# Two layers of adaptive FFN and experts: expert weights split into halves in layer 0 and kept in HBM, conditioning loads merged and moved, routed products on VectorE

## The chip, the cores and the metric

One NeuronCore of one Trainium2 chip runs the whole program. The metric is the device time of one execution, in microseconds.

## What is computed

x is 32 sequences of 64 rows and 512 columns, 2048 tokens. Two residual layers follow each other:

```
x = x + L0_ffn(einsum('bct,bcd->bdt', x, W0[cond_b]))
x = x + L1_ffn(einsum('bct,bcd->bdt', x, W1[subj_b]) + side[subj_b][:, :, None])
```

L0_ffn has a dense FFN of 2048 hidden units with GELU and eight low-rank experts of rank 8 of which each token takes two; each of its two choices has its own hidden activation. L1_ffn has a shared gated FFN of 704 hidden units and eight experts of 352 hidden units, two a token:

```
scores = softmax(x @ gate_w);  topk_w, topk_idx = top_k(scores, 2)
g = silu(einsum('td,edh->teh', x, w_gate)) * einsum('td,edh->teh', x, w_up)
routed = einsum('teh,ehd,te->td', g, w_down, comb)
out = routed + silu(x @ sw_gate) * (x @ sw_up) @ sw_down
```

## The kernel before

The program is written engine by engine. Each engine has its own block with its instructions in order, and semaphores tie the blocks together. An instruction that waits holds everything behind it on its engine. SP only issues DMAs (queue q1). POOL issues DMAs too (queue q0) and does arithmetic.

**Split products.** Matmul operands are kept as two halves, hi (a cast to fp32r) and lo (the value minus hi). A product takes three matmuls: hi by hi, hi by lo, lo by hi. So most data pass a cast (ScalarE mostly) and a subtraction (VectorE or POOL).

**Layer 0** runs over four supers of 512 tokens (s = 0 to 3), and in each over 16 hidden tiles (f). A tile step of TensorE (`step`, L1704) is `hidden` of tile i (14 matmuls), `down` of tile i-1, first half (8), `second` of tile i (2), `down` second half (8). ScalarE does two gelus a tile, `gelu_first` (L894) and `gelu_second` (L900). VectorE does six operations, `hidden_tile` (L1199, L1202 to L1215). `down` waits for g_lo (L1210), `second` for the first gelu. In super 0 the weights come raw from HBM: ScalarE casts (L835), POOL subtracts (`low_w1`, L663), SP stores the split w1 tile to HBM (L505). From super 1 on SP reloads these halves (L513), one tile of 704 KB a step. SP's queue also holds the stores of x1 (L527, at f = 1 of the next super), the loads of xres (L487), of xt halves (L482) and, in super 3, of acc (L516, at f = 4 and 8).

At the turn from super to super VectorE has extra work between tile 0 and tile 1: `add_sums` (L1260) within tile 0 and `add_moved` (L1253) behind it; ScalarE has `move_sums` (L933) between its gelus of tile 1.

After its last `low_w1` POOL loads layer 1's conditioning: 32 matrices of 64 by 64 into `cw1` and 32 columns into `side_col` (`load_matrix`, L444, issues L449 and L452, in a hardware loop at L672). Then it is idle until super 3, where it loads the shared weights (`load_s`, L680).

**Layer 1** first runs the shared FFN over the four supers, with conditioning, gate, top-2 choice and the lists of slots in between. Then comes the routed stage: 39 slot tiles of 128 slots, sorted by expert. `slot_tile` of TensorE is: gate of t+1, `turn_g` of t (three transposes, L1941), up of t+1, `turn_x` of t+2 (four transposes, L1914), `down_routed` of t (L1953, L1954, L1958). Per tile ScalarE does seven operations: xg_hi and xg_f (L1002, L1005), silu (L1012), ru (L1016), rgt_hi and rgt_f (L1020, L1023) and the weighed output yt (L1030). Since POOL cannot read PSUM, xg_f, ru and rgt_f are plain copies of PSUM for it. POOL does `x_low` (L761), `products` (L769) and `g_low` (L773), and between them issues the gather of tile t+5 (L744) and the scatter-add of tile t-1 (L755). A scatter-add waits for the one before to land. VectorE splits the weights of the next expert (`split_expert`, L1469, L1477 to L1491) as soon as the last tile of the expert two before is done; SP loads them raw (`load_expert`, L605), 1408, 512 and 192 KB, when the split before is through.

## Time and profile before

| | us |
|---|---|
| runs | 1054.9, 2602.53, 1051.52 |
| median | 1054.9 |
| the profiled execution | 1050.06 |
| its span | 1048.2 |
| mean granted TensorE clock | 0.993 |

| engine | busy us | share |
|---|---|---|
| TensorE matmul | 1010.6 | 96% |
| TensorE weight load | 837.2 | 80% |
| VectorE | 524.3 | 50% |
| POOL | 354.5 | 34% |
| ScalarE | 314.4 | 30% |

Layer 0 fills the span up to about 540 us, the shared FFN up to about 755, the routed stage the rest. Times in a row are microseconds from the first instruction. In a row of the timeline the bracket gives the idle time of the engine before it and what ended it. A busy TensorE is not TensorE at its peak: the end of a matmul is modelled and overlaps the next one's start, so distances between starts tell the pace.

### The profile page before, as it was taken

What the parts mean: (1) busy time and instruction counts of PE and PEld (TensorE: products, weight loads), DVE (VectorE), ACT (ScalarE), POOL (GpSimd) and SP (SyncE); (2) the same over time, 40 slices, a digit from 0 to 9 for tenths busy, and PEclk for the clock granted to TensorE, in tenths of its full rate; (3) what the DMA queues carried; (4) which work ended last, traced back from release to release, by engine and by line L of the source; (5) the groups of instructions that cost most, each with busy time, mean ns of one, the idle gap of its engine ahead of it and who ended that gap; (6) DMA issues with size and microseconds to landing.
All of it is one profiled execution on the core that took longest, in us unless ns stands there. A gap on an engine that the chain in (4) does not pass through costs nothing.

```text
span 1048.2 us, 14852 instructions
## 1 busy us (share of the span) xinstructions
PE 1010.6 (96%) x4893; PEld 837.2 (80%) x4895; DVE 524.3 (50%) x886; ACT 314.4 (30%) x550; POOL 354.5 (34%) x351
## 2 busy tenths in 40 slices
PE   8899999999999999999999999999989999999993
PEld 5678887888888887888867777778778999999992
DVE  3788777455565455555566333665543314443000
ACT  3743332211121112111242010301144545454541
POOL 4123245410000000000042000022168889898873
PEclk9999999999999999999999999999999999999997
DMA  7387543443433434453444101005155665665433
GB/s 239 130 297 272 161 136 122 166 161 114 140 123 121 153 128 161 142 181 123 138 159 151 41 1 41 1 1 198 58 187 108 163 163 142 141 146 119 80 61 40
DMA packets 51322, 136.41 MB, mean 130 GB/s; under 512 B 8708, under 2 KB 10004, under 8 KB 50772
## 3 DMA queue, kind: packets, MB, share of 16 engines
q1 hardware_dynamic: 36660, 108.15, 30.1%
q0 software_dynamic: 12432, 25.71, 12.4%
q10 hardware_dynamic: 2192, 2.08, 0.7%
q8 instruction: 19, 0.31, 0.1%
q14 instruction: 19, 0.16, 0.0%
HBM read 96.85 MB, written 39.07 MB: 130 GB/s over the span
## 4 chain that ended last, share of the span: by engine, by line
PE 85%; DVE 4%; POOL 4%; DMA 2%; issue 1%; ACT 1%; ACTq 1%; PEldq 0%; POOLq 0%; PEld 0%; DVEq 0%
PE ps_y L1687 6%; PE ps_y L1689 6%; PE ps_y L1688 5%; PE ps_h L1645 5%; PE ps_h L1647 5%; PE ps_h L1646 5%; PE ps_u L1700 3%; PE ps_u L1699 3%; PE ps_h L1933 2%; PE ps_y L1933 2%; PE ps_y L1928 2%; PE ps_y L1929 2%; PE ps_y L1856 2%; PE ps_y L1857 2%; PE ps_h L1840 2%; PE ps_h L1841 2%
## 5 line engine op out<-in xcount | busy, mean ns | idle before, releaser
L1202 DVE TENSOR_TENSOR h<-h,wb 128x512 f32<-128x512 f32 x64 | 44.4, 693 | 162.6 <-ACT h L903 162.5
L897 ACT ACTIVATE h<-ps_h,bias 128x512 f32<-128x512 f32 x64 | 44.0, 689 | 235.1 <-PE ps_h L1654 235.1
L685 POOL DMA_DIRECT2D s_raw<-in_sgu x8 | 4.3, 544 | 299.9 <-DVE g_lo L1210 192.1
L1687 PE MATMUL ps_y<-w_hi,g_hi 128*128 (+1 forms) x256 | 102.2, 399 | 3.5 <-DVE g_lo L1210 3.5
L1689 PE MATMUL ps_y<-w_hi,g_lo 128*128 (+1 forms) x256 | 101.2, 395 | 0.0
L1688 PE MATMUL ps_y<-w_lo,g_hi 128*128 (+1 forms) x256 | 101.0, 395 | 0.0
L1645 PE MATMUL ps_h<-xt_hi,w_hl 128*128 128x512 f32 x256 | 100.0, 391 | 0.7 <-ACT lg_t L846 0.7
L1647 PE MATMUL ps_h<-xt_hi,w_hl 128*128 128x512 f32 x256 | 100.3, 392 | 0.0
L1646 PE MATMUL ps_h<-xt_lo,w_hl 128*128 128x512 f32 x256 | 100.2, 391 | 0.0
L1477 DVE CAST eg_hi<-e_raw 128x704 fp32r<-128x704 f32 x32 | 16.7, 581 | 138.0 <-PE ps_y L1958 125.3
L903 ACT ACTIVATE h<-ps_h,bias 128x512 f32<-128x512 f32 x64 | 43.9, 688 | 115.4 <-PE ps_h L1667 115.4
L755 POOL DMA_INDIRECT out_x<-yt,slot_tok x39 | 62.7, 1607 | 23.3 <-DMA out_x<-yt,slot_tok 12.5
L761 POOL TENSOR_TENSOR xg_lo<-xg_f,xg_hi 128x512 fp32r<-128x512 f32 x39 | 56.3, 1443 | 17.0 <-ACT xg_f L1005 14.9
L1687 PEld LDWEIGHTS ps_y<-w_hi,g_hi 128*128 128x128 f32 x256 | 48.0, 187 | 15.3 <-DVE g_lo L1210 3.5
L1215 DVE TENSOR_TENSOR g_lo<-h,g_hi 128x512 fp32r<-128x512 f32 x64 | 56.9, 888 | 2.2
L1645 PEld LDWEIGHTS ps_h<-xt_hi,w_hl 128*128 128x128 f32 x256 | 48.1, 188 | 12.2 <-ACT lg_t L846 1.2
L1689 PEld LDWEIGHTS ps_y<-w_hi,g_lo 128*128 128x128 f32 x256 | 48.1, 188 | 11.6
L1688 PEld LDWEIGHTS ps_y<-w_lo,g_hi 128*128 128x128 f32 x256 | 48.1, 188 | 11.5 <-issue 0.2
L1646 PEld LDWEIGHTS ps_h<-xt_lo,w_hl 128*128 128x128 f32 x256 | 48.1, 188 | 11.1
L1647 PEld LDWEIGHTS ps_h<-xt_hi,w_hl 128*128 128x128 f32 x256 | 48.1, 188 | 10.4
L773 POOL TENSOR_TENSOR rgt_lo<-rgt_f,rgt_hi 128x384 fp32r<-128x384 f32 x39 | 52.8, 1353 | 6.8 <-ACT rgt_f L1023 6.8
L1928 PE MATMUL ps_y<-eg_hi,xg_hi 128*128 x156 | 53.5, 345 | 0.0
(319 smaller groups left out, 2455.5 us busy)
## 6 DMA issues: line engine op xcount, KB each, us to landing
w_hl<-w1s_d SPq DMA_DIRECT2D x49, 704.0 KB, 4.1
w1s_d<-w_hl SPq DMA_DIRECT2D x16, 704.0 KB, 5.9
e_raw<-in_wgu SPq DMA_DIRECT2D x8, 1408.0 KB, 7.1
w_raw<-in_w1b SPq DMA_DIRECT2D x16, 608.0 KB, 4.7
xres<-in_x SPq DMA_DIRECT2D x16, 256.0 KB, 4.5
acc<-x_d SPq DMA_DIRECT2D x4, 1024.0 KB, 7.6
xc_d<-xc SPq DMA_DIRECT2D x4, 1024.0 KB, 4.8
e_raw<-in_wdn SPq DMA_DIRECT2D x8, 512.0 KB, 8.4
```

Source lines behind the costliest of these rows:

```text
L755: pool.indirect_dma_start(out=out, in_=yt[t % 4][:], in_offset=None, out_offset=bass.IndirectOffsetOnAxis(ap=slot_tok[:, t:t + 1], axis=0) ...
L761: nc.gpsimd.tensor_tensor(xg_lo[:].rearrange("p c n -> p (c n)"), xg_f[:], xg_hi[:].rearrange("p c n -> p (c n)").bitcast(F32), ALU.subtract)\
L773: nc.gpsimd.tensor_tensor(rgt_lo[:].rearrange("p c n -> p (c n)"), rgt_f[:], rgt_hi[:].rearrange("p c n -> p (c n)").bitcast(F32), ALU.sub ...
L1202: tt(h1[u][:], h1[u][:], wb[:, v, :], ALU.mult).then_inc(gch, 1)
L1215: tt(g1_lo[u][:], h1[u][:], g1_hi[u][:].bitcast(F32), ALU.subtract).then_inc(g1_done, 1)
L1645: mm(ps_h[:, u, :], w_chunk(u, 0, c), xt_hi[v][:, c, :], start=(c == 0), stop=False)
L1646: mm(ps_h[:, u, :], w_chunk(u, 0, c), xt_lo[v][:, c, :], start=False, stop=False)
L1647: mm(ps_h[:, u, :], w_chunk(u, 1, c), xt_hi[v][:, c, :], start=False, stop=False)
L1687: mm(ps_y[:, j, :], g_hi[u][:, cols], sl(w2_hi), start=first, **kw)
L1688: mm(ps_y[:, j, :], g_hi[u][:, cols], sl(w2_lo), start=False, **kw)
L1689: mm(ps_y[:, j, :], g_lo[u][:, cols], sl(w2_hi), start=False, **kw)
L1928: mm(o, xg_hi[:, c, :], w(eg_hi, c), start=(c == 0), stop=False)
```

## The change

- **Side column and matrix in one.** The host puts the side column behind each 64-column matrix (`cond1` has 65 columns), so `cw1` has 65 columns and `side_col` is gone. 32 loads instead of 64, two behind each `low_w1` of super 0 on POOL, unrolled.
- **Experts 1 to 7 split ahead.** The host lays each expert's weights out as 6 units of 128 x 768 (`we1`). In supers 1 to 3 one unit goes with each tile step, 42 in all. POOL loads unit k+1 behind the two stores of unit k, ScalarE casts it (`high_unit`, behind the second gelu), VectorE subtracts (`low_unit`, behind the tile), and POOL stores both halves to HBM (`e_d`).
- **SP loads the halves** of expert e from `e_d` straight to where TensorE reads them, 4.46 MB in four DMAs, when the last tile of expert e-2 is done. Expert 1's load stands before the last store of acc. Expert 0 is loaded and split as before.
- **Routed low halves and products on VectorE**, from PSUM. The copies xg_f, ru and rgt_f of ScalarE are gone. POOL only gathers and scatters; scatter t no longer stands behind other work of tile t+1.

The diff, cut:

```diff
-            with pool.Fori(0, J) as j:
                 for h in range(2):
-                    load_matrix(pool, cw1, 1, SEQ, cw1_in[h], j, h)
+                    load_matrix(pool, f, h)
...
+            pool.wait_ge(w1_lo_done, 2 + FT)
+            pool.wait_ge(w2_lo_done, FT)
+            pool.wait_ge(z_ok, 4)
+            def load_unit(k):
+                u = k % 2
+                if k >= 2:
+                    pool.wait_ge(pre_st[u], 32 * (k // 2))
+                at = k % UNITS * UW
+                pool.dma_start(pre_raw[u], we1[k // UNITS, :, at:at + UW]).then_inc(pre_in[u], 16)
+            def store_unit(k):
+                u = k % 2
+                pool.wait_ge(pre_lo_done, k + 1)
+                at = k % UNITS * UW
+                for n, src in enumerate((pre_hi[u].bitcast(F32), pre_raw[u])):
+                    pool.dma_start(e_d[k // UNITS, n, :, at:at + UW], src).then_inc(pre_st[u], 16)
+            load_unit(0)
+            load_unit(1)
+            for k in range(AHEAD):
+                store_unit(k)
+                if 1 <= k < AHEAD - 1:
+                    load_unit(k + 1)
...
+            def high_unit(k):
+                act.wait_ge(pre_in[k % 2], 16 * (k // 2 + 1))
+                nc.scalar.copy(pre_hi[k % 2], pre_raw[k % 2]).then_inc(pre_hi_done, 1)
...
                     gelus(s * FT + f, f, f % 2, s - 1 if f == 1 else None)
+                    if (s - 1) * FT + f < AHEAD:
+                        high_unit((s - 1) * FT + f)
...
+            def low_unit(k, u):
+                dve.wait_ge(pre_hi_done, k + 1)
+                tt(pre_raw[u].bitcast(F32R), pre_raw[u], pre_hi[u].bitcast(F32), ALU.subtract).then_inc(pre_lo_done, 1)
...
                     hidden_tile(s * FT, v, 0, sums=s - 1)
+                    low_unit((s - 1) * FT, 0)
                     add_moved(s - 1)
                     hidden_tile(s * FT + 1, v, 1)
+                    low_unit((s - 1) * FT + 1, 1)
...
                                 hidden_tile(m * 2 + (s * FT + u), v, u)
+                                if (s - 1) * FT + b * 2 <= AHEAD:
+                                    low_unit(m * 2 + ((s - 1) * FT + u), u)
...
+            for s in range(NS - 1):
                 store_acc(s)
+            for u in range(2):
+                sp.wait_ge(pre_st[u], 32 * (AHEAD // 2))
+            sp.wait_ge(gu_done, NS * SH)
+            load_halves(1)
+            store_acc(NS - 1)
             for e in range(1, E):
-                load_expert(e)
+                if e >= 2:
+                    tiles = sp.value_load(last_tile[0:1, e:e + 1], min_val=0, max_val=SLOT_TILES)
+                    sp.wait_ge(ry_done, 1 + tiles)
+                    load_halves(e)
+                sp.wait_ge(half_in, 64 * e)
+                sp.wait_ge(e_done, e)
+                sp.sem_inc(e_done, 1)
...
             for t in range(SLOT_TILES):
-                g_low(t)
-                if t + 1 < SLOT_TILES:
-                    products(t + 1)
-                if t + 2 < SLOT_TILES:
-                    x_low(t + 2)
                 if t + 5 < SLOT_TILES:
                     gather(t + 5)
-                if t:
-                    scatter_add(t - 1)
-            scatter_add(SLOT_TILES - 1)
+                scatter_add(t)
...
+            def x_low(t):
+                dve.wait_ge(xg_hi_done, t + 1)
+                tt(xg_lo[:].rearrange("p c n -> p (c n)"), ps_u[:, 0, :],
+                   xg_hi[:].rearrange("p c n -> p (c n)").bitcast(F32), ALU.subtract).then_inc(xg_lo_done, 1)
+            def products(t, u, first=False):
+                dve.wait_ge(rs_done, t + 1)
+                dve.wait_ge(rup_done, t + 1)
+                if not first:
+                    dve.wait_ge(rgt_done, t)
+                tt(rg[:, 0:H1], rs[:], ps_y[:, u, 0:H1], ALU.mult).then_inc(rg_done, 1)
+            def slot_tile(t, u, nxt=True, nxt2=True):
+                g_low(t)
+                if nxt:
+                    products(t + 1, 1 - u)
+                if nxt2:
+                    x_low(t + 2)
```

## Rows read from the trace of the kernel before

**Rows 1.** The page: busy time, share of the span and instructions of each engine.

```profile
PE 1010.6 (96%) x4893; PEld 837.2 (80%) x4895; DVE 524.3 (50%) x886; ACT 314.4 (30%) x550; POOL 354.5 (34%) x351
```

**Rows 2.** Waits of TensorE, whole span: engine, place, releaser, us in total, times, longest.

```profile
PE ps_u L1914 <- DMA xg<-xc_d,slot_tok: 2.0, 1, 2.0
...
PE ps_h L1933 <- POOL xg_lo L761: 1.0, 6, 0.2
```

**Rows 3.** Windows: stretch, length, busy us by engine, PEclk, DMA share, GB/s.

```profile
750.00:800.00 50.00, 44.38 (x242) 39.14 (x241) 15.93 (x23) 17.95 (x37) 29.88 (x26) 0.97 0.51 155
```

**Rows 4.** Timeline of TensorE: start, duration, line of tiles 2, 3, 6 and 38.

```profile
769.62 0.65 PE L1914 MATMUL ps_u<-ident,xg 128*128 128x128 f32 x4 [2.01 <-DMA xg<-xc_d,slot_tok]
...
777.93 0.60 PE L1914 MATMUL ps_u<-ident,xg 128*128 128x128 f32 x4
...
800.36 0.60 PE L1914 MATMUL ps_u<-ident,xg 128*128 128x128 f32 x4
...
1019.23 0.60 PE L1914 MATMUL ps_u<-ident,xg 128*128 128x128 f32 x4
```

**Rows 5.** Timeline of the tail.

```profile
1028.37 0.69 ACT L1030 ACTIVATE yt<-ps_y,slot_w 128x512 f32<-128x512 f32 x1 [1.71 <-PE ps_y L1958]
...
1033.71 1.58 POOL L755 DMA_INDIRECT out_x<-yt,slot_tok  x1 [2.81 <-DMA out_x<-yt,slot_tok]
1039.49 1.57 POOL L755 DMA_INDIRECT out_x<-yt,slot_tok  x1 [4.21 <-DMA out_x<-yt,slot_tok]
```

**Rows 6.** Timeline of VectorE, routed stage, shortest wait between two experts.

```profile
926.60 2.06 DVE L1477 CAST eg_hi<-e_raw 128x704 fp32r<-128x704 f32 x4 [16.37 <-PE ps_y L1958]
```

**Rows 7.** Groups of POOL: busy us, mean ns | idle before, releaser.

```profile
L665 POOL TENSOR_TENSOR w_hl<-w_raw,w_hl 128x64 fp32r<-128x64 f32 x16 | 10.0, 627 | 88.2 <-ACT w_hl L835 88.2
...
L449 POOL DMA_DIRECT2D cw<-in_cond x32 | 16.7, 521 | 28.8 <-issue 28.8
```

**Rows 8.** Groups of ScalarE and VectorE: the 704-column copy, the 1408-column subtraction.

```profile
L835 ACT CAST w_hl<-w_raw 128x704 fp32r<-128x704 f32 x16 | 12.5, 781 | 10.7 <-PE ps_u L1700 10.7
...
L1233 DVE TENSOR_TENSOR sg_lo<-s_raw,sg_hi 128x1408 fp32r<-128x1408 f32 x2 | 3.2, 1616 | 0.0
```

**Rows 9.** Timeline of a step, last of super 2.

```profile
401.25 0.69 ACT L897 ACTIVATE h<-ps_h,bias 128x512 f32<-128x512 f32 x1 [4.38 <-PE ps_h L1654]
...
404.30 0.69 DVE L1202 TENSOR_TENSOR h<-h,wb 128x512 f32<-128x512 f32 x1 [3.72 <-ACT h L903]
...
406.21 0.69 DVE L1210 TENSOR_TENSOR g_lo<-h,g_hi 128x512 fp32r<-128x512 f32 x1
...
407.20 2.15 POOL L685 DMA_DIRECT2D s_raw<-in_sgu  x4 [192.14 <-DVE g_lo L1210]
...
407.28 0.69 DVE L1215 TENSOR_TENSOR g_lo<-h,g_hi 128x512 fp32r<-128x512 f32 x1
...
408.65 0.69 ACT L897 ACTIVATE h<-ps_h,bias 128x512 f32<-128x512 f32 x1 [4.38 <-PE ps_h L1654]
```

**Rows 10.** DMA from 407 to 413 us, 40 slices of 0.15 us.

```profile
GB/s 113 263 413 338 300 451 413 300 451 488 338 338 225 150 75 150 300 300 413 413 376 338 413 413 375 375 451 301 451 375 375 413 301 338 225 413 451 338 375 222
```

**Rows 11.** DMA issues, KB each, median us to landing.

```profile
w_hl<-w1s_d SPq DMA_DIRECT2D x49, 704.0 KB, 4.1
...
s_raw<-in_sgu POOLq DMA_DIRECT2D x8, 352.0 KB, 3.9
...
out_x<-yt,slot_tok POOLq DMA_INDIRECT x39, 4.9
```

**Rows 12.** Timeline at the turn to super 3.

```profile
421.85 1.29 DVE L1253 TENSOR_TENSOR xres<-zf,xres 128x512 f32<-128x512 f32 x2
...
426.83 0.69 ACT L897 ACTIVATE h<-ps_h,bias 128x512 f32<-128x512 f32 x1 [6.86 <-PE ps_h L1654]
...
428.50 0.39 PE L1666 MATMUL ps_h<-z_step,w_hl 128*128 128x512 f32 x1
```

More of the change, by code:

```diff
@@ L21, with adaln_ffn @@
 LORA_SCALE = 2.0
-def adaln_ffn(nc, x, itok0, itok1, side, cond0, router0, router0_b, w1b, b1, b2, b2s,
-              cond1, gate1, wgu1, wdn1, sgu1, sdn1, out):
+def adaln_ffn(nc, x, itok0, itok1, cond0, router0, router0_b, w1b, b1, b2, b2s,
+              cond1, gate1, wgu1, wdn1, we1, sgu1, sdn1, out):
     N = x.shape[0]
@@ L96, in adaln_ffn @@
                              for u in range(2)])
+        ahead = ExitStack()
+        sb_ahead = tensors(ahead)
+        pre_hi = [sb_ahead(f"pre_hi{u}", [P, UW], F32R)[:] for u in range(2)]
+        pre_raw = [sb_ahead("pre_raw0", [P, UW])[:], u1t[:, 0:UW]]
+        ahead.close()
         w_raw = [sb(f"w_raw{u}", [P, WROW]) for u in range(2)]
@@ L339, in adaln_ffn @@
         out_st = sem("out_st")
+        pre_in = [sem(f"pre_in{u}") for u in range(2)]
+        pre_hi_done = sem("pre_hi_done")
+        pre_lo_done = sem("pre_lo_done")
+        pre_st = [sem(f"pre_st{u}") for u in range(2)]
+        half_in = sem("half_in")
         e_in = sem("e_in")
@@ L783, in _ @@
             nc.gpsimd.memset(rg[:, H1:HC * P], 0.0).then_inc(rg_zero, 1)
-            x_low(0)
-            products(0)
-            x_low(1)
             pool.wait_ge(sy_done, NS * TPS)
@@ L997, in _, with x_high @@
                         rows_step(*rows_step_after_down(s, j))
-            def x_high(t, first=False):
+            def x_high(t):
                 act.wait_ge(xgt_done, t + 1)
                 nc.scalar.copy(xg_hi[:].rearrange("p c n -> p (c n)"), ps_u[:, 0, :]).then_inc(xg_hi_done, 1)
-                if not first:
-                    act.wait_ge(xg_lo_done, t)
-                nc.scalar.copy(xg_f[:], ps_u[:, 0, :]).then_inc(xg_f_done, 1)
             def silu(t, u, first=False):
@@ L1036, in copies @@
                     silu(t + 1, 1 - u)
-                g_high(t, first=stored is None and n == 0)
-                if nxt:
-                    up(t + 1, 1 - u)
+                g_high(t)
                 if nxt2:
@@ L1042, in copies @@
                 weigh(t, n, stored)
-            x_high(0, first=True)
+            x_high(0)
             silu(0, 0, first=True)
-            up(0, 0)
             x_high(1)
@@ L1231, in low_s @@
                     dve.wait_ge(z_done, 2 + STEPS)
+                else:
+                    for u in range(2):
+                        dve.wait_ge(pre_st[u], 32 * (AHEAD // 2))
                 hi, lo, raw = shared_halves(n)
@@ L1271, in diagonals @@
                     nc.vector.tensor_copy(bdq[u][rows, :, h * SEQ:(h + 1) * SEQ],
[L1272 removed]
+                                          cw1[rows, s * TPS:(s + 1) * TPS, 0:SEQ]).then_inc(bdq_done, 1)
             def split_gate():
@@ L1544, in _, with g_low @@
                             split_expert(0, 0, k)
-            for e in range(1, E):
-                dve.wait_ge(e_in, 48 * (e + 1))
-                if e >= 2:
-                    tiles = dve.value_load(last_tile[0:1, e:e + 1], min_val=0, max_val=SLOT_TILES)
-                    dve.wait_ge(ry_done, 1 + tiles)
-                for k in range(4):
-                    split_expert(e, e % 2, k)
+            def x_low(t):
[8 more added lines that the diff above has]
+                tt(rg[:, 0:H1], rs[:], ps_y[:, u, 0:H1], ALU.mult).then_inc(rg_done, 1)
+            def g_low(t):
+                dve.wait_ge(rgt_hi_done, t + 1)
+                tt(rgt_lo[:].rearrange("p c n -> p (c n)"), ps_u[:, 1, 0:HC * P],
+                   rgt_hi[:].rearrange("p c n -> p (c n)").bitcast(F32), ALU.subtract).then_inc(rgt_lo_done, 1)
+            def slot_tile(t, u, nxt=True, nxt2=True):
[4 more added lines that the diff above has]
+                    x_low(t + 2)
+            x_low(0)
+            products(0, 0, first=True)
+            x_low(1)
+            for t in range(2):
+                slot_tile(t, t)
+            with dve.Fori(1, (SLOT_TILES - 2) // 2) as m:
+                for u in range(2):
+                    slot_tile(m * 2 + u, u)
+            for t in range((SLOT_TILES - 2) // 2 * 2, SLOT_TILES):
+                slot_tile(t, t % 2, t + 1 < SLOT_TILES, t + 2 < SLOT_TILES)
         @block.tensor
```

89 lines of the change are left out of this document (34 added, 55 removed).

## The prediction

> **What bounds the kernel now.** I read the page's busy times first: TensorE is busy 1010.6 us, 96% of a span of 1048.2 [rows 1]. The reader is to see that the kernel is TensorE's own work from end to end. An edit elsewhere can win only what TensorE waits for, plus the stretch behind its last matmul. The waits of TensorE name few such places. The two that matter here lie in layer 1's routed stage: 2.0 us for a gather, and 1.0 us in six pieces for POOL's low half of x [rows 2]. The stretch from 750 to 800 us lies there too: TensorE busy 44.38 of 50 us and the granted clock 0.97 [rows 3]. So the routed stage can give a little. Layer 0 can give nothing, but it can be made worse.
>
> The profiled execution took 1050.06 us, 1.9 above its span, and all sums are made on it. The median of the three runs is 1054.9 (the others are 1051.5 and a disturbed 2602.5), so the profiled run lies 1.5 to 4.8 us below its neighbours.
>
> **Layer 1, what goes.** Three terms.
>
> First, tile 2. Its transposes wait 2.01 us for the gather [rows 4], because POOL issues gathers 2 to 4 only behind its arithmetic for tiles 0 and 1. In the new order POOL has no arithmetic there and already stands at its wait for the last shared tile, so these gathers go out sooner by several microseconds. Gain 2.0. The next interval, 769.62 to 777.93, is 8.31 us, where a steady one is 6.71 to 6.78, mean 6.745. It lies behind the gap, in the stretch with the reduced clock [rows 3]; without the gap I take the loss of 1.6 to be gone.
>
> Second, the 35 intervals from 777.93 to 1019.23 last 241.3 us [rows 4]. 35 steady ones would be 236.1, so 5.2 are lost. The interval that ends at 800.36 lasts 8.92 us and has 2.2 of it: POOL was late there with the low half of g, behind its first scatters. The six waits for x_low [rows 2] go with intervals of 7.1 to 7.2, 0.43 too long each, 2.6. VectorE now makes low halves and products straight from PSUM, and nothing else runs on it: 512, 384 and 352 columns at 0.7 us or less each (a subtraction of 512 columns takes 0.69 [rows 9]), about 1.9 us of 6.7. ScalarE drops three of its seven operations a tile. Gain 4.5; the rest stands at the loop's turns, where nothing changes.
>
> Third, the tail. yt of tile 37 is ready at 1029.06, yet its scatter goes at 1033.71 and the last one at 1039.49 [rows 5]. One scatter frees the next after 5.8 us (their distance), and the chain is late because scatter t-1 stands behind tile t's arithmetic on POOL. With only gathers and scatters in that queue, 37 goes at 1029.3 and 38 at 1035.1, 4.4 us sooner; the product of tile 38 comes before that. What follows the last issue stays.
>
> Sum of layer 1: 2.0 + 1.6 + 4.5 + 4.4 = 12.5 us. Bounds: nothing, if each place gets a new wait; 15, if the turns of the loop give theirs too and the clock somewhat more.
>
> **Layer 1, what is added.** Each expert after the first comes as two halves, 4.46 MB, where 2.16 MB came raw; VectorE's split of it is gone. From one release to the next VectorE splits for 11 us and then idles 16.4 at the least [rows 6], 27.4 together. At 0.37 MB/us (below) the halves take 12 us and 2 fixed, with scatters between perhaps 16. They are there 11 us before use, which covers them: cost 0; were the cover gone, up to 5 us an expert. SP waits in this loop, and only its final waits are queued behind. For expert 1, SP loads before the last store of acc; that store waits for shared sums that end some 14 us after the loads can start, so they are about through, and the first scatter, which waits for the store, now has a free POOL.
>
> **Layer 0, first super.** POOL idles 88.2 us in all before its 16 low halves, 5.5 each [rows 7]. The 64 conditioning loads become 32, each 0.52 us to issue and 28.8/32 = 0.9 of value load and addresses before it [rows 7], 2.8 us a step for two. That idle time hides them: cost 0. Without it the low half of w1 would reach TensorE late by up to 2.8 us in some 14 steps. The other end, a gain, is excluded: nobody waited for these loads.
>
> **Layer 0, supers 1 to 3: 42 units.** A tile step there now also has a copy of 768 columns on ScalarE; 704 took 781 ns [rows 8], so 0.85 us. On VectorE it has a subtraction of 768 columns: 1408 took 1616 ns [rows 8], 512 took 0.69 us [rows 9], 1.03 ns a column between, so 0.96. A step lasts 7.39 us (ScalarE's first gelus, 401.25 and 408.65). VectorE starts a tile at 404.30, ends it at 407.97 and starts the next at 411.7 [rows 9]: 0.96 fits into 3.7 of idle. ScalarE has 4.4 us between its second gelu, which releases VectorE at 404.30, and the next first one at 408.65. By busy time both additions are free.
>
> But the units also form a ring: low(k) on VectorE, two stores and then the load of k+1 on POOL, its landing, high(k+1) on ScalarE, low(k+1). ScalarE works in order, so behind a late load all its gelus wait, then VectorE's tile and TensorE. POOL starts 0.30 us after VectorE ends (407.20 against 406.90) and takes 0.54 an issue [rows 9]. For the transfer, four POOL loads of 352 KB issued from 407.20 on moved 1.44 MB; 3.9 after its issue [rows 11] at 408.8 the last has landed, 5.5 from the first issue. The rate was some 0.37 MB/us [rows 10]. Our three hold 1.18 MB, so 5.5 - 0.26/0.37 = 4.8 us. SP's reload of 0.72 MB takes 4.1 [rows 11]; by size that makes 4.1 + 0.46/0.37 = 5.3. No row has a store on POOL's queue. From below it is the 4.1 of the smaller transfer; from above, the three one after another, 3 x 3.9 = 11.7. I take 4.8, because the four loads are nearest in kind: same queue, same issue, overlapping. The ring is 0.3 + 4.8 + 0.1 + 0.85 + 0.05 + 0.96 = 7.06 us against a step of 7.39. In an ordinary step low ends at 408.9, the stores start at 409.2, the load lands at 414.0, the copy ends at 414.9, and the next gelu wants ScalarE at 416.04: 1.1 us to spare, and 0.98 more before TensorE feels it (the gelu of 426.83 ends at 427.52, its reader runs at 428.50) [rows 12]. Cost 0. With 5.3 the ring is 7.56 and costs 0.17 a step, 6 us.
>
> The cover is thin in these places:
> - The turns to supers 2 and 3. Low(32) starts at 421.85, where add_moved stood [rows 12]. It pushes the next tile by 0.96, some 0.3 of it felt by TensorE, and the load of unit 33 goes out only at 424.2. It lands at 427.9, with the 1 MB store of x1 beside it up to 429.3. The copy ends at 428.8 to 430.1, and the gelu of 426.83 is 2.0 to 3.3 late, less 0.98: 1.0 to 2.3. With the 0.3 that is 2.0 a turn, 4.0.
> - The 1 MB acc load of super 3 beside a unit: 1.0.
> - The x1 store after the turn to super 1, beside unit 2: 1.0.
>
> Sum of layer 0: +6.0, its bounds 0 and, by the 11.7, +6.6 a step or +250; the upper end has no row near it in kind, and I let the ring's rival below stand for it.
>
> The Trainium skill ("SBUF — State Buffer", on who interferes with whom) says that GpSimd cannot write the descriptors of its DMAs while VectorE copies fp32 from SBUF to SBUF in a two-port mode. By this rule three issues that met VectorE's two casts would lose about a microsecond, and a small slip of the ring would become a lasting one. In the rows of before VectorE idles from 407.97 to 411.7, where the issues will stand, and casts only behind that; no row shows a DMA issue beside a cast in layer 0.
>
> **Forecast.** 1050.06 - 12.5 + 6.0 = 1043.6 us on the basis of the profiled run, 1048.4 on that of the median. I give the middle, 1046.
>
> **The rivals.**
> - The ring binds (slower). Place: the load of each unit in supers 1 to 3. It decides from 5.1 us between first issue and landing, where the ring passes 7.39, and each further microsecond costs 38 us over some 38 steps. For it: the 5.3 by SP's rows, and two thirds of the bytes being writes. Against: the four loads of POOL's own queue. At 6.2 it is + 42 - 12.5: 1080.
> - The turns are covered (faster). Landing in 4.4, the big stores yielding, layer 0 costs 1: 1050.1 - 12.5 + 1 = 1038.6.
> - The halves crowd the scatters. A scatter lands in 4.9 us [rows 11] and each waits for the last. Were that doubled for 14 of 27 us, the chain would fall behind by more than the 6.7 - 5.8 = 0.9 us a tile that it can win back, and the four yt buffers would hold ScalarE, then TensorE: 3 us for each of 5 experts, 1058.6. Against: the chain has the POOL queue to itself.
>
> **Chances.** Forecast 0.58 (its own range 1040 to 1053), ring 0.16, turns covered 0.18, scatters 0.08. A measurement of this kernel can tell about 2%, 21 us, from no change. TensorE's idle time is 38 us in all, start and tail included, so faster by over 2% has hardly a way: 0.03. Slower by over 2% is most of the ring's case: 0.12. Within: 0.85. The range reaches from the covered case with 3.6 us to spare, 1035, to a ring that binds by half a microsecond (1043.6 + 19, and the offset of the median), 1067.
>
> **What would show it.** Right: no wait for the gather of tile 2; intervals of 6.71 to 6.78 from 770 to 1020 but for the loop's turns; the last scatter issued 6 us after yt 37; steps of 7.39 between 320 and 400; waits for h0 only near the turns, 1 to 2 us each. Wrong: steps over 7.39 with ScalarE's copy released by DMA in each (ring), or yt released by the scatters throughout (third rival). The forecast falls if layer 0 costs over 15 us or layer 1 wins under 6.

## The result, and the profile after

The changed kernel takes 1072.1 us (median; 1071.3 to 1073.6), the kernel before 1053.8 in the same session. The ratio is 1.0183, with a 95% interval from 1.0157 to 1.0208: slower by 19 us. A few executions were disturbed, as one of 2602.5 us of the kernel before; medians count them and ratios leave them out. The forecast was 1046, its range ended at 1067. Experiments below are compared by their ratio to the kernel before on their own chip, whose median there was 1050 to 1052. Differences "by the ratios" are differences of ratios times 1051 us.

The profiled execution took 1072.57 us, with a span of 1071.0. First the page's busy times, the row that answers to [rows 1].

```profile
PE 1022.7 (95%) x4893; PEld 846.1 (79%) x4895; DVE 555.9 (52%) x947; ACT 296.4 (28%) x475; POOL 267.0 (25%) x327
```

TensorE has as many matmuls as before but is busy for 12.1 us more. The same work took longer, and the mean granted clock is 0.978 where it was 0.993. VectorE has the units in layer 0 and the products of layer 1, and POOL has lost its arithmetic. None of the three helpers is over 52% busy. Where TensorE waits is in its waits, which answer to [rows 2] (engine, place, releaser, us in total, times, longest):

```profile
PE ps_h L1716 <- ACT h L915: 11.5, 5, 4.1
PE ps_u L1749 <- ACT m_base L876: 8.4, 2, 8.1
```

Both are in layer 0, and but for 0.9 us of the first line both are new. The five waits of the first line stand at the first GELU (`gelu_first`) of a tile, the long one of the second at the copy of a mask. The waits of the routed stage for the gather and for POOL's xg_lo are gone.

**Where the time went.** A ruler for layer 0 is the second GELU of each tile, 63 starts in ScalarE's timeline (L903 before, L921 after). From first to last it is 478.3 us before and 513.2 after, so layer 0 lost 34.9 us. Their intervals place it: start of super 0 1.5; turn to super 1 4.5; turn to super 2 12.0; turn to super 3 7.1; tiles 6 to 8 of super 3 7.5; the rest, 2.3, in pieces at the ends of supers and at tile 12 of super 3. At tile 12 TensorE waits 0.98 us for a reload of w_hl by SP, the one place of layer 0 where it waits for other traffic. Most ordinary steps still last 7.39. A further 1.7 us went between the layers. Layer 1 gained: from its first turn of x to the end of the span it takes 13.8 us less. 34.9 + 1.7 - 13.8 = 22.8 is the difference of the spans.

**An ordinary step.** ScalarE's and POOL's timelines in super 1 (start, us, engine, line, operation, idle before and its releaser):

```profile
225.23 0.84 ACT L932 CAST pre_hi<-pre_raw 128x768 fp32r<-128x768 f32 x1 [3.16 <-DMA pre_raw<-in_we]
226.46 0.69 ACT L915 ACTIVATE h<-ps_h,bias 128x512 f32<-128x512 f32 x1 [0.38 <-PE ps_h L1704]
...
232.72 0.83 ACT L932 CAST pre_hi<-u1t 128x768 fp32r<-128x768 f32 x1 [3.25 <-DMA u1t<-in_we]
...
240.24 0.84 ACT L932 CAST pre_hi<-pre_raw 128x768 fp32r<-128x768 f32 x1 [3.38 <-DMA pre_raw<-in_we]
241.24 0.69 ACT L915 ACTIVATE h<-ps_h,bias 128x512 f32<-128x512 f32 x1 [0.16 <-PE ps_h L1704]
```

```profile
227.36 0.54 POOL L712 DMA_DIRECT2D e_d<-pre_hi  x1 [5.88 <-DVE pre_raw L1231]
227.89 0.54 POOL L712 DMA_DIRECT2D e_d<-pre_raw  x1
228.42 0.54 POOL L705 DMA_DIRECT2D u1t<-in_we  x1
```

The load is issued at 228.42 and ScalarE copies at 232.72: 4.3 us, or 5.36 from the first store. The copies come every 7.49 to 7.52 us, so the ring (load, copy, subtraction, stores, next load) is 0.1 us longer than the step. TensorE does not feel it yet. The first GELU's idle time behind the copy shrinks from 0.38 to 0.16 us in two steps, and the slack is gone when the super ends.

**The turn to super 2.** Compare [rows 12], the same kind of turn before. VectorE, POOL, ScalarE and TensorE, in that order:

```profile
306.61 0.95 DVE L1231 TENSOR_TENSOR pre_raw<-pre_raw,pre_hi 128x768 fp32r<-128x768 f32 x1
```

```profile
307.86 0.54 POOL L712 DMA_DIRECT2D e_d<-pre_hi  x1 [10.73 <-DVE pre_raw L1231]
...
308.92 0.54 POOL L705 DMA_DIRECT2D u1t<-in_we  x1
```

```profile
304.62 0.69 ACT L921 ACTIVATE h<-ps_h,bias 128x512 f32<-128x512 f32 x1 [0.84 <-PE ps_h L1717]
313.26 0.83 ACT L932 CAST pre_hi<-u1t 128x768 fp32r<-128x768 f32 x1 [7.95 <-DMA u1t<-in_we]
314.00 0.58 ACT L876 CAST m_base<-ps_u 128x512 bf16<-128x512 f32 x1
...
323.34 0.69 ACT L915 ACTIVATE h<-ps_h,bias 128x512 f32<-128x512 f32 x1 [8.28 <-PE ps_h L1704]
```

```profile
314.63 0.80 PE L1749 MATMUL ps_u<-g_hi,w_hl 128*128 128x512 f32 x1 [8.12 <-ACT m_base L876]
```

Read it as a chain. Tile 0's sums keep VectorE busy, so low(16) starts only at 306.61. Load 17 stands behind it on POOL. ScalarE is in order and stands at high_unit(17) for 7.95 us, and the copies of the next super's masks stand behind that. They are copied out of a bank of PSUM that TensorE's `down` of tile 0 writes next, so TensorE cannot go on. After the gap the clock is lower (windows: stretch, length, busy us by engine, PEclk, DMA share, GB/s):

```profile
310.00:315.00 5.00, 0.37 (x1) 0.38 (x2) 3.19 (x6) 1.74 (x3) 0.00 (x0) 0.56 0.50 157
315.00:320.00 5.00, 5.00 (x13) 3.89 (x13) 0.08 (x1) 0.06 (x1) 1.61 (x3) 0.50 0.69 231
320.00:325.00 5.00, 5.00 (x21) 4.02 (x20) 0.00 (x0) 0.69 (x1) 0.00 (x0) 0.91 0.93 254
```

0.50 is the 1.2 GHz level. Matmuls start 0.43 us apart there and 0.235 at 2.4 GHz; the slow stretch lasts from 314.63 to 320.8 and costs some 2.8 us. The wait of 8.1, these 2.8 or so and 0.7 at tile 1 make the 12.0.

**The turn to super 3** has the same chain with another reader. ScalarE's copy, then TensorE:

```profile
450.32 0.83 ACT L932 CAST pre_hi<-u1t 128x768 fp32r<-128x768 f32 x1 [10.52 <-DMA u1t<-in_we]
```

```profile
451.79 0.80 PE L1716 MATMUL ps_h<-z_step,w_hl 128*128 128x512 f32 x1 [3.95 <-ACT h L915]
```

The load went out at 442.97, beside SP's 1 MB store of x1 (443.21), and took 7.35 us. At the turn to super 2 that store stood on SP behind a reload of w_hl, which waits for TensorE, and went out only at 319.71; the load took 4.3 there. No masks are left to copy, so the first GELU of tile 2 is what TensorE misses.

**Tiles 6 to 8 of super 3.** POOL in the changed kernel, then in e3, a kernel of below in which neither ScalarE nor VectorE works on units:

```profile
488.35 0.54 POOL L712 DMA_DIRECT2D e_d<-u1t  x1 [2.61 <-issue]
488.88 0.54 POOL L705 DMA_DIRECT2D pre_raw<-in_we  x1
```

```profile
467.71 0.54 POOL L713 DMA_DIRECT2D e_d<-u1t  x1 [2.62 <-issue]
```

The second store of unit 37 goes out 2.6 us behind the first, and nothing in the profile holds it. It does so in e3, e4 (there the first store), e5, e8 and e12 as well, at the same unit, so the delay belongs to a place in POOL's list and not to the ring. What it is stays open. The load behind it, issued at 488.88, lands in 6.0 us, the load before it (476.67, beside SP's loads of acc and xres) in 6.4. TensorE then waits 4.15 us.

**The routed stage.** The window that answers to [rows 3], then turns of x for [rows 4]:

```profile
787.00:837.00 50.00, 48.18 (x282) 44.52 (x282) 15.54 (x28) 13.02 (x25) 16.80 (x14) 1.00 0.49 134
```

```profile
803.25 0.60 PE L1964 MATMUL ps_u<-ident,xg 128*128 128x128 f32 x4
810.03 0.60 PE L1964 MATMUL ps_u<-ident,xg 128*128 128x128 f32 x4
...
1046.01 0.60 PE L1964 MATMUL ps_u<-ident,xg 128*128 128x128 f32 x4
```

35 intervals in 235.98 us, each 6.71 or 6.78; no wait for a gather, a granted clock of 1.00 in the window. The tail answers to [rows 5], here POOL's last scatters:

```profile
1056.84 1.55 POOL L800 DMA_INDIRECT out_x<-yt,slot_tok  x1 [3.88 <-DMA out_x<-yt,slot_tok]
1062.30 1.55 POOL L800 DMA_INDIRECT out_x<-yt,slot_tok  x1 [3.91 <-DMA out_x<-yt,slot_tok]
```

From the last turn of x to the last scatter's issue it is 16.3 us, where it was 20.3.

### The profile page after: what moved, and what is told of

The parts are those of the page before. It is cut to its first block and busy times, and to the rows that moved or that the text cites. A ratio compares the mean times of both kernels' runs of the same rounds, so it can differ in the third digit from the quotient of the medians.

```text
span 1071.0 us, 14838 instructions
## 1 busy us (share of the span) xinstructions
PE 1022.7 (95%) x4893; PEld 846.1 (79%) x4895; DVE 555.9 (52%) x947; ACT 296.4 (28%) x475; POOL 267.0 (25%) x327
## 5 line engine op out<-in xcount | busy, mean ns | idle before, releaser
L1737 PE MATMUL ps_y<-w_hi,g_hi 128*128 (+1 forms) x256 | 104.7, 409 | 2.3 <-DVE g_lo L1222 2.3
L1739 PE MATMUL ps_y<-w_hi,g_lo 128*128 (+1 forms) x256 | 103.8, 405 | 0.0
L1738 PE MATMUL ps_y<-w_lo,g_hi 128*128 (+1 forms) x256 | 103.6, 405 | 0.0
L712 POOL DMA_DIRECT2D e_d<-pre_hi x42 | 22.8, 542 | 298.6 <-DVE pre_raw L1231 168.0
L1584 DVE TENSOR_TENSOR rgt_lo<-ps_u,rgt_hi 128x384 fp32r<-128x384 f32 x39 | 21.8, 558 | 139.8 <-ACT rgt_hi L1038 139.8
L921 ACT ACTIVATE h<-ps_h,bias 128x512 f32<-128x512 f32 x64 | 43.9, 688 | 104.1 <-PE ps_h L1717 104.1
L1749 PE MATMUL ps_u<-g_hi,w_hl 128*128 128x512 f32 x128 | 52.0, 406 | 8.4 <-ACT m_base L876 8.4
L1697 PEld LDWEIGHTS ps_h<-xt_hi,w_hl 128*128 128x128 f32 x256 | 48.7, 190 | 10.6
L1978 PE MATMUL ps_h<-eg_hi,xg_hi 128*128 x156 | 50.4, 324 | 1.8 <-ACT xg_hi L1026 0.9
```

The lines of the kernel that those rows point to most:

```text
L1697: mm(ps_h[:, u, :], w_chunk(u, 1, c), xt_hi[v][:, c, :], start=False, stop=False)
L1737: mm(ps_y[:, j, :], g_hi[u][:, cols], sl(w2_hi), start=first, **kw)
L1738: mm(ps_y[:, j, :], g_hi[u][:, cols], sl(w2_lo), start=False, **kw)
L1739: mm(ps_y[:, j, :], g_lo[u][:, cols], sl(w2_hi), start=False, **kw)
L1749: mm(ps_u[:, half, :], a2, hi[u][:], start=first, **kw)
L1978: mm(o, xg_hi[:, c, :], w(eg_hi, c), start=(c == 0), stop=False)
```

## The experiments

The theory, called T1 in the expectations: layer 0's loss is the place of the load of unit k+1, behind low(k) and its stores, together with ScalarE's order at the turns. R1: the traffic itself. R2: the added instructions. R3: the clock alone. R4, of e7 and e10: copies and landings together crowd something else. A summary first; "layer 0" is the ruler of above.

| kernel | median us | ratio to before, 95% | layer 0, us |
|---|---|---|---|
| before | 1050 to 1054 | 1 | 478.3 |
| changed | 1072.1 | 1.0183 (1.0157 to 1.0208) | 513.2 |
| e1, no units | 1038.8 | 0.9891 (0.9859 to 0.9923) | 478.3 |
| e2, arithmetic alone | 1038.5 | 0.9899 (0.9870 to 0.9928) | 479.2 |
| e3, transfers alone | 1036.0 | 0.9867 (0.9843 to 0.9892) | 478.1 |
| e4, load ahead of stores | 1055.4 | 1.0044 (1.0016 to 1.0072) | 496.4 |
| e5, masks ahead of unit | 1065.4 | 1.0122 (1.0095 to 1.0150) | 510.2 |
| e7, third buffer | 1043.7 | 0.9924 (0.9904 to 0.9943) | 485.3 |
| e8, half the bytes | 1056.8 | 1.0050 (1.0030 to 1.0069) | 499.6 |
| e10, e7 with e4's order first | 1041.7 | 0.9909 (0.9883 to 0.9935) | 481.6 |
| e12, e8 with e5 | 1052.6 | 1.0009 (0.9991 to 1.0027) | 493.4 |
| e9, e1, products back | 1075.3 | 1.0219 (1.0193 to 1.0246) | 478.3 |
| e11, e9 with two loads | 1047.5 | 0.9959 (0.9944 to 0.9975) | 478.7 |

### e1: no units

```diff
-            load_unit(0)
-            load_unit(1)
-            for k in range(AHEAD):
...
-                        high_unit((s - 1) * FT + f)
-                    low_unit((s - 1) * FT, 0)
...
-                                 e_d[e - 1, k, :, 0:gu]).then_inc(half_in, 16)
+                                 we1[e - 1, :, 0:gu]).then_inc(half_in, 16)
```

> The changed kernel without any unit in layer 0: no loads or stores of units on POOL, no copy of a unit on ScalarE, no subtraction on VectorE. The halves of an expert are both loaded from the input in layer 1 (same bytes, same places), so the low halves are wrong values at the same cost. Theory T1 (the whole loss of 34 to 36 us up to the end of layer 0 comes from the units; layer 1 keeps its gain of about 13.8): about 1072 - 35 + 1.5 (the start of super 0, which the units do not touch) = 1037 to 1041, ratio to before 0.985 to 0.988, and the last second GELU of layer 0 at 525 to 527 against 560.1. If part of the loss belongs to the conditioning loads moved into super 0, layer 0 ends later than 527 by that part.

Measured: 1038.8, layer 0 exactly as before. So the whole loss is the units', and the conditioning loads in super 0 cost nothing; the 1.5 us at the start in the changed kernel's profile belongs to that execution (in the other kernels that start takes from 0.3 us less to 0.5 more than before). What the rest of the change is worth is 1.1%, about 11.5 us.

### e2: the units' arithmetic alone

```diff
             load_unit(0)
             load_unit(1)
-            for k in range(AHEAD):
...
-                act.wait_ge(pre_in[k % 2], 16 * (k // 2 + 1))
+                act.wait_ge(pre_in[k % 2], 16)
+                if k >= 2:
+                    act.wait_ge(pre_lo_done, k - 1)
```

> The changed kernel with the units' arithmetic alone: ScalarE's 42 copies and VectorE's 42 subtractions stay in their places, the two unit buffers are loaded once, and nothing is stored or loaded again (the copies then work on what is in the buffers). Layer 1 as in e1. T1 (the late landings at the turns are the loss, the added instructions cost nothing by themselves): 1038 to 1043, and no PE wait over 2 us on ScalarE in supers 1 to 3. Rival R2 (the added instructions, 0.85 and 0.96 us a step, make ScalarE and VectorE late at the turns): the waits of 4 to 8 us at the turns stay at half their size or more, 1055 to 1070.

### e3: the units' transfers alone

```diff
-                        high_unit((s - 1) * FT + f)
-                    low_unit((s - 1) * FT, 0)
...
-                pool.wait_ge(pre_lo_done, k + 1)
+                pool.wait_ge(g1_done, 2 + FT + k + 1)
+                pool.wait_ge(pre_in[u], 16 * (k // 2 + 1))
```

> The changed kernel with the units' transfers alone: POOL stores and loads each unit at the same point of the step (now paced by the end of VectorE's work on the hidden tile), same bytes and queue, but no copy and no subtraction of units, so nobody on ScalarE or VectorE waits for a landing. Layer 1 as in e1. T1: 1038 to 1043, since the traffic of 130 to 180 GB/s by itself delays nothing that the chain waits for. Rival R1 (the traffic slows other transfers, the w_hl loads and the x1 and acc transfers, and these make PE late): 1050 to 1070, with PE waits on DMA or SP in place of those on ScalarE.

Measured: 1038.5 and 1036.0. TensorE's largest wait on ScalarE in layer 0, in e2 and in e3:

```profile
PE ps_h L1709 <- ACT h L909: 0.9, 1, 0.9
```

```profile
PE ps_h L1711 <- ACT h L916: 0.9, 1, 0.9
```

Each part alone is free to within 1 us by the ruler, and both together cost some 31 us by the ratios. That refutes R1 and R2. R3 falls too as a cause of its own: without the waits the mean granted clock is 0.995 and 0.994. What is left is the coupling: ScalarE waits for a landing, and the landing's issue waits for VectorE.

### e4: the load ahead of the stores

```diff
             for k in range(AHEAD):
-                store_unit(k)
                 if 1 <= k < AHEAD - 1:
                     load_unit(k + 1)
+                store_unit(k)
```

> The changed kernel with two lines exchanged on POOL: the load of unit k+1 is issued before the two stores of unit k instead of behind them (it needs only the stores of unit k-1 landed, which were issued a step earlier). All work and bytes are the same. T1 (the loss is the place of the load behind low(k) and the two stores): the load now starts about 3 us or more earlier and lands before ScalarE wants it, the waits at the turns to supers 2 and 3 go, 1038 to 1046, ratio 0.986 to 0.992. R1 or R2 (traffic or added work as such): no more than 5 us better than the changed kernel, 1067 or more. R3 (only the lower clock behind the gaps would be worth much): it falls with the gaps and cannot be told apart here; e2 and e3 say whether the gaps are from the chain of landings.

Measured: 1055.4, by the ratios 15 us better than the changed kernel, but 16 short of e1: a miss for the number T1 gave. POOL's timeline shows why, in super 1 and at tile 1 of super 3; the row from the DMA issues behind it has KB each and median us to landing.

```profile
276.29 0.55 POOL L705 DMA_DIRECT2D pre_raw<-in_we  x1 [6.22 <-DMA e_d<-pre_raw]
276.83 0.54 POOL L712 DMA_DIRECT2D e_d<-pre_hi  x1
...
446.67 0.54 POOL L705 DMA_DIRECT2D u1t<-in_we  x1 [7.48 <-DMA e_d<-u1t]
```

```profile
e_d<-pre_raw POOLq DMA_DIRECT2D x21, 384.0 KB, 5.7
```

A load may go only when the stores of its buffer have landed. Those stores now go out right behind a load, and the second lands in 5.7 us, where the changed kernel has 3.8. So the stores of each unit start when those of the last have landed: a second chain, of 8 us and more where it is slow (276.29 to the next load at 284.61), took the place of the first.

### e5: the masks ahead of the unit

```diff
+                    if s + 1 < NS and f == 1:
+                        masks(s + 1)
                     if (s - 1) * FT + f < AHEAD:
                         high_unit((s - 1) * FT + f)
-                    if s + 1 < NS and f == 1:
-                        masks(s + 1)
```

> The changed kernel with one exchange on ScalarE: at tile 1 of supers 1 and 2 the two copies of the next super's masks (L876) are issued ahead of the copy of the unit instead of behind it. e4 has shown that no order of waits alone brings all back; this one asks how much of the turn to super 2 (12.0 us late in the changed kernel) is the masks' place. T1: PE's wait of 8.1 us on the mask goes, the turn costs what the late load leaves for the first GELU of tile 2 (some 3 to 5 us), so 4 to 8 us in all are gained: 1064 to 1068, ratio 1.010 to 1.014 against 1.0183. Rival: the masks only uncovered a late load that makes the first GELU just as late, within 2 us of the changed kernel.

Measured: 1065.4, as expected. (The profiled execution, of 1067.4 us, was the slowest of the four.) ScalarE at the turn to super 2:

```profile
304.64 0.58 ACT L876 CAST m_base<-ps_u 128x512 bf16<-128x512 f32 x1
...
315.74 0.83 ACT L932 CAST pre_hi<-u1t 128x768 fp32r<-128x768 f32 x1 [10.04 <-DMA u1t<-in_we]
316.48 0.68 ACT L915 ACTIVATE h<-ps_h,bias 128x512 f32<-128x512 f32 x1
```

The mask is 9.4 us earlier and its wait is gone. The two intervals of the turn fall from 28.45 us to 22.90 (before: 17.22). What is left is the late load itself, now before the first GELU, and it is later than it was: with TensorE's gap gone, SP's 1 MB store of x1 goes out at 308.70 beside the load (308.35), which now takes 7.39 us. Layer 0 as a whole takes only 3.0 us less by the ruler, 1.5 of it at the start. In this profile ordinary steps at the ends of supers 1 and 2 last 7.5 to 7.8 too (3.6 us in all), and tiles 6 to 8 of super 3 cost 10.5: there the ring binds outside the turns.

### e7: a third raw buffer

```diff
+        pre_raw = [..., u1t[:, 0:UW], u1t[:, UW:2 * UW]]
+        raw_of = lambda k: pre_raw[k % 2 if k < 10 else (k - 10) % 3]
...
             for k in range(AHEAD):
                 store_unit(k)
-                if 1 <= k < AHEAD - 1:
+                if 1 <= k <= 10:
                     load_unit(k + 1)
+                if 10 <= k < AHEAD - 2:
+                    load_unit(k + 2)
```

> A third raw buffer for the units (the next 768 columns of u1t, free once the base and step rows of super 2 are placed), from unit 12 on; POOL then issues the load of unit k+2 behind the stores of unit k, so each load has two steps of 7.39 us to land and each pair of stores more than one, where e4 took its load's time from the stores. The tile loops of VectorE in supers 1 to 3 are written out for it. T1 (two chains of landings, of the load and of the stores, each a step long with two buffers, are the whole loss): from super 2 on no PE wait over 2 us, the turn to super 1 keeps up to 4.5 us of its loss; 1038 to 1045, ratio 0.987 to 0.993, the best of the kernels with units. Rival R4 (copies and landings together crowd something else, e.g. stores that VectorE's casts hold back on POOL's queue): 1050 or more, with waits of ScalarE on DMA still over 5 us.

Measured: 1043.7, the first kernel with units that beats the kernel before. TensorE's waits:

```profile
PE ps_h L1725 <- ACT h L922: 3.1, 3, 1.9
```

Every byte, every copy and every subtraction of the changed kernel is present here, and so is the order store, then load; what changed is how far ahead a load goes. (VectorE's tile loops had to be written out for it, which no run has alone; in e2 the loops are there and cost nothing.) The turns to supers 2 and 3 cost 0.3 us each in their first interval, and 0.8 follows the first of them. 4.2 us stay at the turn to super 1, where the third buffer is not free yet. The late store of unit 37 is still late, and costs 0.45. This, with e2 and e3, shows T1.

### e8: half the bytes

```diff
-                pool.dma_start(pre_raw[u], we1[k // UNITS, :, at:at + UW])
+                w = UW if k < 2 else UW // 2
+                pool.dma_start(pre_raw[u][:, 0:w], we1[k // UNITS, :, at:at + w])
...
-                    pool.dma_start(e_d[k // UNITS, n, :, at:at + UW], src)
+                    pool.dma_start(e_d[k // UNITS, n, :, at:at + UW // 2], src[:, 0:UW // 2])
```

> The changed kernel, every wait and instruction in place, but each unit's load (from unit 2 on) and both its stores carry only the first half of the columns, 192 KB in place of 384 KB (so the halves of layer 1 are read from the input, as in e1). T1 (the ring is as long as the landing from issue): the landing falls from 4.3 us by 1 to 2 us, the ring to 5.5 to 6.5 us against the step of 7.39, the turns find slack, and three quarters of the loss or more goes: 1038 to 1048. Rival (a wait's place costs the same whatever the size, since it is the fixed part of a landing): 1058 or more.

Measured: 1056.8, between the two expectations; T1's number was too good. The landing fell from 4.3 to 3.0 us, and the ring is shorter than the step. But the turn to super 2 is nearly as bad as with whole units, because there the load's place counts more than its size. ScalarE, then POOL:

```profile
306.31 0.83 ACT L933 CAST pre_hi<-u1t 128x768 fp32r<-128x768 f32 x1 [7.17 <-DMA u1t<-in_we]
307.05 0.58 ACT L877 CAST m_base<-ps_u 128x512 bf16<-128x512 f32 x1
```

```profile
303.26 0.54 POOL L706 DMA_DIRECT2D u1t<-in_we  x1
```

Of 7.17 us at most 3.05 are the landing; for the rest the load is not issued yet, since it stands behind low(16) and its stores.

### e12: half the bytes and the masks ahead

Edit: that of e8 and that of e5 together.

> e8 (units' transfers of half the size) with e5's exchange (masks of the next super ahead of the unit on ScalarE). e8 left one large loss, the turn to super 2 (19.25 us where the kernel before has 9.83), with PE waiting 7.3 us for the mask. T1: that wait goes, and with it 6 to 9 us of e8's 1056.8: 1047 to 1051, about the sum of what e5 and e8 gain by themselves. Rival: the first GELU of tile 2 is as late as the masks were, within 3 us of e8.

Measured: 1052.6, 4 us off e8: less than T1's 6 to 9, more than the rival's 3. The turn to super 2 went from 19.25 us to 13.65 and then gave 1.6 of it back in the next interval, since the load of unit 17 now delays the first GELU. POOL and ScalarE:

```profile
302.54 0.54 POOL L706 DMA_DIRECT2D u1t<-in_we  x1
```

```profile
309.14 0.83 ACT L933 CAST pre_hi<-u1t 128x768 fp32r<-128x768 f32 x1 [9.77 <-DMA u1t<-in_we]
```

SP's store of x1 goes out at 302.46, just ahead of the load. Beside it 192 KB take 6.6 us, where they take 3.0 in most steps. Here the neighbour does more to the landing than the load's own size. Two turns and tiles 6 to 8 of super 3 make the 15 us that stay.

### e10: e7 with e4's order in super 1

```diff
             for k in range(AHEAD):
-                store_unit(k)
                 if 1 <= k <= 10:
                     load_unit(k + 1)
+                store_unit(k)
                 if 10 <= k < AHEAD - 2:
                     load_unit(k + 2)
```

> e7 with the order of e4 up to unit 10: there POOL issues the load of unit k+1 ahead of the stores of unit k, since the third buffer is not free yet; from unit 12 on as in e7. In e7 what was left of the loss was the turn to super 1 (intervals of 10.06, 9.94 and 8.55 us where the kernel before has 9.54, 7.39 and 7.39), in e4 that turn cost 10.06, 7.39, 7.39. T1: about 3 us off e7 (1043.7), 1040 to 1042, ratio 0.989 to 0.991, within 2 us of e1's ratio of 0.989. Rival R4 (the stores' serial landings in super 1 cost as much as they save): within 1 us of e7.

Measured: 1041.7, ratio 0.9909, the fastest of those that keep the whole computation. By the ruler it is 3.7 us better than e7 and within 3.3 us of e1. The ratios of e7 and e10 overlap, so that e10 is the faster rests on the ruler of one profile each, and on its waits:

```profile
PE ps_h L1725 <- ACT h L922: 0.9, 1, 0.9
```

### e9: products back on POOL and ScalarE

```diff
             for t in range(SLOT_TILES):
+                g_low(t)
+                if t + 1 < SLOT_TILES:
+                    products(t + 1)
+                if t + 2 < SLOT_TILES:
+                    x_low(t + 2)
                 if t + 5 < SLOT_TILES:
                     gather(t + 5)
-                scatter_add(t)
+                if t:
+                    scatter_add(t - 1)
+            scatter_add(SLOT_TILES - 1)
```

ScalarE's copies xg_f, ru and rgt_f are back as well, and VectorE has no routed work.

> e1 (no units in layer 0, halves of layer 1 loaded) with the routed stage's products and low halves back as in the kernel before: low halves and products on POOL, the copies for them on ScalarE. It asks whether the gain of layer 1 (13.8 us by the traces) is the move to VectorE or the splits that VectorE no longer makes. By the prediction (all four terms come from the chain that runs through POOL and its queue): the tile interval is back at 6.89 us and the last scatters behind the last products, so 10 to 13 us slower than e1, ratio to before 0.999 to 1.003. Rival (the splits on VectorE and their loads were what held the tiles): within 4 us of e1, ratio up to 0.993.

Measured: 1075.3, ratio 1.0219: 34 us slower than e1 by the ratios, some three times what the dearer theory gave. POOL, then TensorE:

```profile
813.29 1.59 POOL L795 DMA_INDIRECT out_x<-yt,slot_tok  x1 [5.17 <-DMA out_x<-yt,slot_tok]
814.34 1.57 POOL L813 TENSOR_TENSOR rgt_lo<-rgt_f,rgt_hi 128x384 fp32r<-128x384 f32 x1
```

```profile
815.97 1.65 PE L1999 MATMUL ps_y<-ed_hi,rgt_lo 128*128 x3 [3.29 <-POOL rgt_lo L813]
```

SP's four loads of an expert go out from 799.91 to 801.24. A scatter beside them lands so late that POOL waits 5.17 us for it, and rgt_lo stands behind that wait. TensorE waits 3.29, and with the low clock after it the interval is 12.75 us. There are six such intervals, one for each expert's load beside running tiles. All others from the third on are 6.68 to 6.78, although the products are on POOL.

### e11: the same with two loads

```diff
-                    load_halves(e)
-                sp.wait_ge(half_in, 64 * e)
+                    if e == 2:
+                        load_halves(e)
+                sp.wait_ge(half_in, 64 * min(e, 2))
```

> e9 (products and low halves on POOL and ScalarE, no splits on VectorE) with only the halves of experts 1 and 2 loaded; experts 3 to 7 use what is in the buffers, so five of the six loads beside running tiles are gone. In e9 six tile intervals were 11.7 to 12.7 us, each behind a load. If a load's crowding of a scatter that POOL waits for ahead of rgt_lo is the cause: one such interval left, about 5 x 5.8 = 29 us off e9's 1075.3, so 1044 to 1048 (e1 plus the later last scatters, some 4 us, plus the one interval). Rival (POOL's products are slower than VectorE's as such, and the loads only mark the places): 1060 or more.

Measured: 1047.5, as expected. TensorE's wait and the window behind it:

```profile
PE ps_y L2000 <- POOL rgt_lo L814: 3.1, 1, 3.1
```

```profile
814.00:819.00 5.00, 5.00 (x16) 4.64 (x17) 0.00 (x0) 0.69 (x1) 4.53 (x4) 0.50 0.43 99
```

One interval of 12.80 us is left. A wait of 3.1 cost 12.80 - 6.75 = 6.1: about half of it is the clock. Layer 1 takes 11.4 us more than in e1 by the traces. The other parts are the tail, 28.8 us from the last turn of x to the end of the span against 24.8, and 1.3 in the first two intervals, where POOL's arithmetic is.

## Why the prediction was wrong, point by point

- **Layer 1, removed (12.5).** Right in its sum: 13.8 by the traces, 11.5 by e1. Steady intervals (235.98 for a forecast 236.1) and tail (4.0 for 4.4) came as priced. The cause given for the first two terms was mostly wrong, though. I put the gather's wait and the 4.5 us on POOL's arithmetic ahead of gathers and scatters. e9 and e11 have that arithmetic in its place. Their gathers 2 to 4 go out as late as before, yet of the 2.0 us of wait 0.4 is left in e11, and no interval away from a load is over 6.8. What they lack is VectorE's splits and the raw loads (gathers 2 to 4 land in a median of 3.6 us in e11, 4.3 in the kernel before). For the six waits for x_low the splits stand in the trace of before. POOL and VectorE ahead of the first of them:

```profile
809.26 1.94 POOL L761 TENSOR_TENSOR xg_lo<-xg_f,xg_hi 128x512 fp32r<-128x512 f32 x1
```

```profile
809.97 1.85 DVE L1485 CAST ed_hi<-e_raw 128x512 fp32r<-128x512 f32 x2
```

  x_low takes 1.93 to 1.95 us at all six and 1.28 or 1.29 at most other tiles. Which part the loads had is not isolated. By e9 and e11 the move of the products itself gives the tail, 4.0, and 1.3 in the first two intervals; the other 8.5 went with the splits and raw loads. That my sum came out near was in this part luck.
- **Layer 1, added (0).** Right: the halves of an expert land within 14.6 to 17.6 us of the first issue, ahead of their use. But in the changed kernel too, a scatter beside a load holds POOL for over 8 us:

```profile
844.96 1.59 POOL L800 DMA_INDIRECT out_x<-yt,slot_tok  x1 [8.02 <-DMA out_x<-yt,slot_tok]
850.93 1.59 POOL L800 DMA_INDIRECT out_x<-yt,slot_tok  x1 [3.07 <-DMA out_x<-yt,slot_tok]
```

  The third rival's mechanism is therefore there, six times, and no tile interval shows it: on POOL only gathers, five tiles ahead, still stand behind a scatter, and the chain catches up at 5.7 us a scatter. The doubled loads need the move of the products for this: with them on POOL five such loads cost 27 us (e9 against e11).
- **Conditioning loads (0).** Right: e1's layer 0 takes what it took before, 478.3 us.
- **Sizes of the added instructions.** Right: 0.83 on ScalarE and 0.96 on VectorE for 0.85 and 0.96, and all but free by themselves (0.9 us in e2).
- **The landing (4.8).** Mis-sized: 5.4 from the first issue, by my own upper estimate from SP's reload. The ring is 7.5 us, not 7.06. In an ordinary step this cost nothing at once, but it ate the slack of 1.1 us that I carried into each turn.
- **The turns (2.0 each).** This step failed, and it decided the result: they cost 12.0 and 7.1, in a layer 0 that was put at +6.0 and measured +34.9. The time at which the load goes out was right (2.3 us behind the start of low, as forecast). Three things behind it were missing. I followed the load only to the next GELU and did not list what stands behind high_unit(f=1) on ScalarE. At the turn to super 2 these are the copies of the masks, whose PSUM bank TensorE needs in the same tile (e5: 5.5 us at the turn). I took the landing beside the store of x1 at 3.7 us, or 5.1 if the store held it; it was 7.35 at the turn to super 3, and 7.39 in e5 at the turn to super 2. And I priced a wait at its own length, where the reduced clock behind it takes some 3 us more.
- **Other places (1.0 each).** The turn to super 1 cost 4.5: unit 2's load took 8.5 us there. Tiles 6 to 8 of super 3 cost 7.5: landings of 6.4 and 6.0 us where others take 4.3, and between them the store that comes 2.6 us late, whose cause stays open.
- **The rival "ring binds"** had the mechanism, and was wrong in its form. It asked whether the ring is longer than the step everywhere, with 38 us for each microsecond. At 5.4 that rule gives 11 us, spread evenly. The loss came instead in lumps, where low comes late or the load lands beside a large transfer of SP. e8 tells the two apart: with the ring well under a step the lump at the turn stays. e5's profile, with 3.6 us in ordinary steps, shows that the even form is near.
- **The Trainium skill's rule** ("SBUF — State Buffer", on who interferes with whom), by which VectorE's casts hold up GpSimd's descriptors, found no case in ordinary steps: POOL's issues (227.36 to 228.96) stand in VectorE's idle time there. Where a cast does meet one (220.22, with a store issued at 220.41), the issue takes 0.54 us and the load behind it lands in 4.3, as elsewhere. The Trainium skill has one that would have pointed the right way ("DMA: Bandwidth & Descriptors", rules for kernel authors): issue a DMA early and wait for it late. e7 against the changed kernel agrees, with 27 us by the ratios.

Still not isolated by a run: how the 7.5 us in super 3 divide between the delayed store and the slow landings. In e8 and e12, with short landings elsewhere but the same delay, 4.5 and 4.3 us of them stay.

## What to carry to other kernels

Work spread into the idle time of two engines is free only while neither has to wait for the other: here arithmetic alone and transfers alone cost at most 1 us, and joined by a ring of two buffers they cost 31. Price such a ring at its worst step, not its mean one: find the step in which the producer's part comes last (here the turn), add the landing beside whatever large transfer is due there, and list every instruction behind the waiting one in its engine's order. If that sum passes the step, try one more buffer, with the load a step further ahead: here it won 27 us, and the two exchanges of order 15 and 6.

## What was not expected of the hardware

- A wait of TensorE of 8.12 us was followed by about 6 us at half clock (0.50 in 315 to 320 of the changed kernel), one of 3.1 by about 5 (0.50 in 814 to 819 of e11), and it cost 6.1. Even one of 1.88 (e7, ending at 195.04) was followed by half clock up to about 198.5, and the tiles there lost 3.7 us.

```profile
195.00:197.00 2.00, 1.96 (x5) 1.58 (x6) 0.46 (x2) 0.69 (x1) 1.32 (x3) 0.54 0.12 49
```

- A scatter of one tile, 5.3 to 6.0 us from its issue to that of the next when it is alone and the chain is behind, takes 10.6 to 11.4 beside four loads on SP's queue (4.46 MB in all).
- In the changed kernel the second of two 384 KB stores on POOL's queue lands in 3.8 us, in e4, behind a load, in 5.7. The load takes 4.2 to 4.3 us from its own issue in both.
- A POOL load beside SP's 1 MB store of x1 took 7.35 us for 384 KB (changed kernel, 442.97) and 6.6 for 192 KB (e12, 302.54), where the medians are 4.3 and 3.0.
